# Two unused row gathers by GpSimd, placed late in a top-k search

## The chip, the cores and the metric

The kernel runs on one core of one Trainium2 chip. The metric is the device time of one execution in microseconds (us); lower is better. The core has five engines that run their own instruction streams and meet only at semaphores: TensorE (PE, with its weight loads PEld), VectorE (DVE), ScalarE (ACT), GpSimd (POOL) and SyncE (SP).

## The reference, cut to what matters

B=4 sequences of T=1024 tokens with C=256 channels go through a cross attention over 64 context tokens, and then through a layer of 8 experts in which each expert picks its own 256 tokens in each sequence:

```python
x = x + xattn(_layernorm(x), ctx, Wq, bq, Wk, bk, Wv, bv)
x = x + ffn(_layernorm(x), gate_w, w1, w2)

def ffn(x, gate_w, w1, w2):
    cap = int(2.0 * T / E)                      # 256
    probs = softmax(einsum('BTC,CE->BTE', x, gate_w))
    top_p, top_idx = lax.top_k(transpose(probs, (0, 2, 1)), cap)
    xin = take_along_axis(x[:, None], top_idx[..., None], axis=2)
    h = gelu(einsum('BElC,ECH->BElH', xin, w1), approximate=False)
    y = einsum('BElH,EHC->BElC', h, w2) * top_p[..., None]
    return zeros((B, T, C)).at[b_idx, top_idx].add(y)
```

## The kernel before, in words

The program has three stages.

**Attention (0 to about 52 us).** Eight groups of 512 tokens (`NG`) pass through scores, softmax and weighted values. The sum x + attention stays in the SBUF tile `x_all` and is stored to the output.

**Search and listing (about 58 to 86 us).** For each of 4 x 8 sequence-expert pairs the kernel finds the 256th largest probability by a search in 10 rounds of 3 bits each (`ROUNDS` is 5, run over the upper and then the lower bits), in two halves `h` of two sequences. A round goes back and forth between two engines: DVE compares all keys with 7 candidates (`compare`, line 1190, writes `over`), PE counts (line 872), DVE thresholds the count (`keep_reached`, line 1196), PE adds the new floor (line 880), DVE makes the next candidates (`candidates`, line 1201, writes `cand` and raises the semaphore `cand_ready[h]`). `candidates(0, ...)` is called four times in each block of five rounds, eight times in all. In the same stretch ACT normalises the rows, SP stores them to the DRAM scratch `xn_rows` (line 447, four DMAs, semaphore `xn_stored`), and ACT and DVE prepare the weights of expert 0 (`w1hi`, `w1lo`, `w2both`). Then DVE turns the thresholds into a list of row numbers `gidx` for expert 0 (lines 1294 to 1350).

**Experts (about 87 to 477 us).** Each expert works on 8 tiles of 128 rows, in two groups `g` of NL=4 tiles. GpSimd gathers the rows of a group by indirect DMA from `xn_rows` into `xg[g]` (line 525), PE turns them (line 750) into a PSUM bank, ACT and DVE split them into a high and a low part (`xhi`, `xlo`), PE multiplies with `w1` (lines 932 and 994) and `w2` (lines 944 to 953), and GpSimd adds the results to the output by indirect DMA (line 533). For the very first group the work starts on two of the four tiles: PE waits for `first_gathered` (2 tiles), later for the other two.

Every engine's order is the order in which the code issues; there is no scheduler. On GpSimd an instruction that waits holds up all that stands behind it on that engine. Between the setting of its last small tile (`own_base`, line 541) and its first gather GpSimd has two waits, for `xn_stored` and for `gidx_ready`, and nothing to do:

```python
pool.wait_ge(xn_stored, 16 * B)
pool.wait_ge(gidx_ready, 1)
for g in range(NU):
    gather(g, FIRST if g == 0 else 0)
```

On PE `keep_warm` issues transposes whose result nobody reads: 20 after the first list, 8 after the second ranking, 6 after the first turned rows.

Of the kernel before, what the change touches and what calls it, by code (L numbers as in the profile page):

```python
# [28 lines left out]
I32 = mybir.dt.int32  # L29
# [5 lines left out]
P = 128  # L35
# [10 lines left out]
def build(nc, x, xT, ctxT_in, Wq, WkT, Wv, WvT, bv, small, w1, w2, out):  # L46
    B, T, C = x.shape
    S = ctxT_in.shape[1] // B
    E, _, H = w1.shape
    CAP = 2 * T // E  # L50
    TC = T // P
# [19 lines left out]
    ROUNDS = BITS // RB  # L71
# [14 lines left out]
    out_v = out.rearrange("b (p c) d -> p b c d", c=TC)  # L86
    xn_v = xn_dram.rearrange("(b p c) d -> p b c d", b=B, c=TC)
    out_rows = out.rearrange("b t d -> (b t) d")

    with ExitStack() as stack:  # L90
        def sb(name, shape, dt):
            return stack.enter_context(nc.sbuf_tensor(name, shape, dt))

        def sem(name):
            return stack.enter_context(nc.semaphore(name))
# [81 lines left out]
        tok_val = sb("tok_val", [P, B, NB, TC], F16)  # L177
        onehot = sb("onehot", [P, B, SL, TC], F16)
        gidx = sb("gidx", [P, NB], I32)
        own = sb("own", [P, B, NB], F32)  # L180
        own_base = sb("own_base", [P, 1], F32)
        own_tok = sb("own_tok", [P, NB, B], F32)
# [6 lines left out]
        xg = [sb(f"xg{g}", [P, NL, CX], F32) for g in range(NU)]  # L189
# [46 lines left out]
        rows_stored = sem("rows_stored")  # L236
        rows_added = sem("rows_added")
        settled = sem("settled")
        xn_stored = sem("xn_stored")
        soft = sem("soft")  # L240
        normed = sem("normed")
# [9 lines left out]
        cand_ready = [sem(f"cand_ready{h}") for h in range(2)]  # L251
# [44 lines left out]
        pool_passed = sem("pool_passed")  # L296

        def keep_wait(eng, passed):

            eng.sem_inc(passed, 1)  # L300
# [162 lines left out]
        def _(pool):  # L463
# [23 lines left out]
            for r in range(ROUNDS):  # L487
# [3 lines left out]
                      channel_multiplier=0).then_inc(steps_set, 1)  # L491
# [36 lines left out]
            def scatter(g, e):  # L528
                for i in range(NL):
# [3 lines left out]
                    pool.indirect_dma_start(out=out_rows, out_offset=at, in_=ysb[g][:, i, :], in_offset=None,  # L533
                                            compute_op=ALU.add).then_inc(rows_added, 16)

            pool.memset(own[:], 0.0).then_inc(own_set, 1)
            pool.wait_ge(own_set, 1)
            for b in range(B):
                at = slice(b * SL, (b + 1) * SL)
                pool.memset(own[at, b], 1.0).then_inc(own_set, 1)  # L540
                pool.memset(own_base[at, :], float(b * T)).then_inc(own_set, 1)

            pool.wait_ge(xn_stored, 16 * B)
            pool.wait_ge(gidx_ready, 1)
            for g in range(NU):
# [959 lines left out]
```

## Time and profile before

| | us |
|---|---|
| median of 3 runs | 482.37 |
| lowest and highest of these | 482.18 and 506.92 |
| the profiled execution, its whole time | 479.12 |
| its span, from the first to the last instruction | 477.4 |

In the profiled execution 1.7 us lie around the span. Times of instructions below are from the start of the span. An indirect DMA of GpSimd shows in the engine's row only as long as GpSimd writes its descriptors; the time from issue to landing is another row. Matmuls are pipelined, so neighbouring PE rows overlap a little.

### The profile page before, as it was taken

Reading aid. Unit: us, or ns where it says so; the run is one execution under the profiler, and the core shown is the slowest. Engines: PE = TensorE matmul, PEld = TensorE weight load, DVE = VectorE, ACT = ScalarE, POOL = GpSimd, SP = SyncE. Lnnn points to the kernel's source line nnn. Section 1 sums busy time; section 2 is a strip of 40 time slices with the busy share of each in tenths; the row PEclk is TensorE's granted clock in tenths of the full one; section 3 lists DMA queues with packets and bytes.
Section 4 is the critical chain, followed back from the end, with each engine's and each line's share of the span. In section 5 each row is a group of like instructions: output and inputs, shape, how many; then the busy total and the mean of one; then the engine's idle time right before and its main releaser. Section 6 shows DMA issues by size and latency. Waiting matters only on the chain.

```text
span 477.4 us, 8390 instructions
## 1 busy us (share of the span) xinstructions
PE 443.9 (93%) x2600; PEld 376.3 (79%) x2600; DVE 317.9 (67%) x813; ACT 212.6 (45%) x523; POOL 198.4 (42%) x222
## 2 busy tenths in 40 slices
PE   8999344799999999999999999999999999999993
PEld 7887233788888888888888888888888888888993
DVE  3888798784677467746774677467656765674551
ACT  2478698042554255424532453345234524442331
POOL 4544400510835182518252815281538153814242
PEclk9999755799999999999999999999999999999998
DMA  8984844241425351625161517150715081504142
GB/s 275 362 279 154 287 185 183 57 157 55 80 56 152 72 80 50 178 53 78 45 194 42 84 34 212 30 84 28 219 34 78 23 220 38 85 12 45 13 49 29
DMA packets 35667, 52.46 MB, mean 110 GB/s; under 512 B 3009, under 2 KB 28994, under 8 KB 35138
## 3 DMA queue, kind: packets, MB, share of 16 engines
q1 hardware_dynamic: 22946, 34.89, 21.9%
q0 software_dynamic: 12288, 17.08, 21.1%
q10 hardware_dynamic: 416, 0.27, 0.2%
q8 instruction: 9, 0.15, 0.1%
q14 instruction: 8, 0.07, 0.0%
HBM read 35.17 MB, written 16.92 MB: 109 GB/s over the span
## 4 chain that ended last, share of the span: by engine, by line
PE 88%; DVE 8%; POOL 1%; ACT 1%; issue 1%; POOLq 0%; DVEq 0%
PE bank L932 37%; PE wide L949 23%; PE wide L953 12%; PE bank L750 4%; PE bank L811 3%; DVE over L1190 3%; PE wide L836 3%; PE wide L944 2%; PE bank L907 1%; DVE cand L1201 1%; DVE x_all L1106 1%; PE bank L755 1%; PE bank L994 1%; DVE w1lo L1370 1%; POOL rs L511 1%
## 5 line engine op out<-in xcount | busy, mean ns | idle before, releaser
L949 PE MATMUL wide<-w2both,hhi 128*128 128x512 f32 x480 | 176.1, 400 | 0.0
L533 POOL DMA_INDIRECT out_dram<-ysb,sidx x64 | 104.4, 1631 | 115.4 <-DVE ysb L1381 90.6
L689 ACT ACTIVATE hraw<-bank 128x512 f32<-128x512 f32 (+1 forms) x136 | 77.7, 571 | 132.6 <-PE bank L932 128.2
L953 PE MATMUL wide<-w2both,hlo 128*128 128x256 f32 x480 | 134.3, 280 | 0.0
L525 POOL DMA_INDIRECT xg<-xn_rows,gidx x64 | 65.5, 1023 | 132.3 <-issue 81.2
L1362 DVE CAST hhi<-hraw 128x512 fp32r<-128x512 f32 (+1 forms) x136 | 57.9, 425 | 79.4 <-ACT hraw L689 77.6
L949 PEld LDWEIGHTS wide<-w2both,hhi 128*128 128x128 f32 x480 | 90.5, 188 | 19.3
L1364 DVE TENSOR_TENSOR hlo<-hraw,hhi 128x512 fp32r<-128x512 f32 (+1 forms) x136 | 90.3, 664 | 4.7
L953 PEld LDWEIGHTS wide<-w2both,hlo 128*128 128x128 f32 x480 | 90.3, 188 | 3.5
L932 PE MATMUL bank<-xlo,w1hi 128*128 128x512 f32 (+1 forms) x268 | 80.5, 381 | 0.0
L932 PE MATMUL bank<-xhi,w1lo 128*128 128x512 f32 (+1 forms) x268 | 80.2, 380 | 0.0
L932 PE MATMUL bank<-xhi,w1hi 128*128 128x512 f32 (+1 forms) x268 | 79.9, 379 | 0.0
L932 PEld LDWEIGHTS bank<-xlo,w1hi 128*128 128x128 f32 x268 | 49.3, 188 | 10.3
L932 PEld LDWEIGHTS bank<-xhi,w1lo 128*128 128x128 f32 x268 | 49.3, 188 | 9.9
L932 PEld LDWEIGHTS bank<-xhi,w1hi 128*128 128x128 f32 x268 | 42.1, 188 | 5.6 <-ACT hraw L689 0.2
L682 ACT ACTIVATE xhi<-bank 128x512 fp32r<-128x512 f32 x30 | 18.0, 600 | 62.1 <-PE bank L750 62.1
L1354 DVE TENSOR_TENSOR xlo<-bank,xhi 128x512 fp32r<-128x512 f32 x30 | 20.8, 692 | 33.1 <-ACT xhi L682 31.7
L672 ACT ACTIVATE w2both<-raw 128x256 fp32r<-128x256 f32 x64 | 26.1, 417 | 23.3 <-PE wide L953 23.3
L1375 DVE TENSOR_TENSOR w2both<-raw,w2both 128x256 fp32r<-128x256 f32 x64 | 26.5, 420 | 4.8 <-ACT w2both L672 4.4
L1370 DVE TENSOR_TENSOR w1lo<-raw,w1hi 128x256 fp32r<-128x256 f32 x64 | 26.4, 422 | 0.0
L669 ACT ACTIVATE w1hi<-raw 128x256 fp32r<-128x256 f32 x64 | 25.8, 414 | 0.0
L1381 DVE SCALAR_TENSOR_TENSOR ysb<-wide,pcol,ysb 128x256 f32<-128x256 f32 x60 | 24.8, 477 | 0.0
(178 smaller groups left out, 435.3 us busy)
## 6 DMA issues: line engine op xcount, KB each, us to landing
raw<-in_w_dram SPq DMA_DIRECT2D x16, 1024.0 KB
xn_rows<-x_all SPq DMA_DIRECT2D x4, 1060.0 KB, 3.9
x_all<-in_x_dram SPq DMA_DIRECT2D x8, 512.0 KB, 9.6
raw<-in_x_turned_dram SPq DMA_DIRECT2D x8, 512.0 KB, 9.3
out_dram<-x_all SPq DMA_DIRECT2D x8, 512.0 KB, 4.9
xg<-xn_rows,gidx POOLq DMA_INDIRECT x64, 3.2
out_dram<-ysb,sidx POOLq DMA_INDIRECT x64
ctxT<-in_ctx_turned_dram ACTq DMA_DIRECT2D x1, 256.0 KB, 3.6
```

Of the source, the lines that this page charges most:

```text
L525: pool.indirect_dma_start(out=xg[g][:, i, :], out_offset=None, in_=xn_dram, in_offset=at).then_inc(first_gathered if i < first else gather ...
L533: pool.indirect_dma_start(out=out_rows, out_offset=at, in_=ysb[g][:, i, :], in_offset=None, compute_op=ALU.add).then_inc(rows_added, 16)
L669: act.activation(w1hi[:, j], w1raw[:, :, bass.ts(j, P)], ACT.Copy).then_inc(w1_hi, 1)
L672: act.activation(w2hi[:, j], w2raw[:, j], ACT.Copy).then_inc(w2_hi, 1)
L689: act.activation(hraw[s % 2][:, 0:width], bank[s % 2][:, 0:width], ACT.Gelu).then_inc(gelu_done, 1)
L932: t = pe.matmul(bank[s % 2][:, 0:width], w[:, j, k, :], xx[g][:, k, cols], start=(m == 0), stop=(m == 5))
L949: return pe.matmul(y[:, 0:2 * C], hhi[s % 4][:, at], w2both[:, j].rearrange("p a d -> p (a d)"), start=(j == 0), stop=(j == HC - 1), skip_ ...
L953: return pe.matmul(y[:, 0:C], hlo[s % 4][:, at], w2hi[:, j, :], start=False, stop=False, skip_group_check=True)
L1362: dve.tensor_copy(hhi[s % 4][:, 0:width], hraw[s % 2][:, 0:width]).then_inc(h_hi, 1)
L1364: dve.tensor_tensor(hlo[s % 4][:, 0:width], hraw[s % 2][:, 0:width], hhi[s % 4][:, 0:width].bitcast(F32), ALU.subtract).then_inc(h_split, 1)
L1370: dve.tensor_tensor(w1lo[:, j], w1raw[:, :, bass.ts(j, P)], w1hi[:, j].bitcast(F32), ALU.subtract).then_inc(w1_split, 1)
L1375: dve.tensor_tensor(w2lo[:, j], w2raw[:, j], w2hi[:, j].bitcast(F32), ALU.subtract).then_inc(w2_split, 1)
```

## The change

GpSimd sets a new tile `row_no` of 128 row numbers (0 to 127). After the small tiles it waits until that is set and until `cand_ready[0]` has reached 2 * (ROUNDS - 1) - 1 = 7, that is, until the seventh of the eight calls of `candidates(0, ...)` is done. Then it issues two indirect DMAs. Each gathers the rows 0 to 127 of the input x (1 KB each, 128 KB a DMA) into the first 256 columns of a slot of `xg[1]`, the buffer that the real gathers of the second group fill later. Nobody reads what the two have fetched. GpSimd then waits for both to land (`tried_out`), and only then stands before the two waits that it had already.

```diff
+    x_rows = x.rearrange("b t d -> (b t) d")
...
+        row_no = sb("row_no", [P, 1], I32)
...
+        row_set = sem("row_set")
+        tried_out = sem("tried_out")
...
+            pool.iota(row_no[:], [[0, 1]], base=0, channel_multiplier=1).then_inc(row_set, 1)
             pool.memset(own[:], 0.0).then_inc(own_set, 1)
             pool.wait_ge(own_set, 1)
             for b in range(B):
...
+            pool.wait_ge(row_set, 1)
+            pool.wait_ge(cand_ready[0], 2 * (ROUNDS - 1) - 1)
+            keep_wait(pool, pool_passed)
+            for i in range(2):
+                pool.indirect_dma_start(out=xg[1][:, i, 0:C], out_offset=None, in_=x_rows,
+                                        in_offset=bass.IndirectOffsetOnAxis(ap=row_no[:], axis=0)).then_inc(tried_out, 16)
+            pool.wait_ge(tried_out, 32)
             pool.wait_ge(xn_stored, 16 * B)
             pool.wait_ge(gidx_ready, 1)
             for g in range(NU):
```

GpSimd's instructions in the kernel before, from the last factor of the second normalisation to its first gathers; `[waits ...]` names the semaphores that hold a row up:

```order
L511 TENSOR_TENSOR rs<-ve,neghalf 128x2 [waits var2]
L536 MEMSET own 128x32
L540 MEMSET own 32x8 [waits own_set]
L541 MEMSET own_base 32x1
...
L525 DMA xg<-xn_rows,gidx 128x265 [waits xn_stored,gidx_ready]
L525 DMA xg<-xn_rows,gidx 128x265 x7
```

The same place on GpSimd in the changed kernel, whose lines are numbered up to 4 higher there:

```order
L515 TENSOR_TENSOR rs<-ve,neghalf 128x2 [waits var2]
L540 IOTA row_no 128x1
L541 MEMSET own 128x32
L545 MEMSET own 32x8 [waits own_set]
L546 MEMSET own_base 32x1
...
L552 DMA xg<-in_x_dram,row_no 128x256 [waits row_set,cand_ready0]
L552 DMA xg<-in_x_dram,row_no 128x256
L529 DMA xg<-xn_rows,gidx 128x265 [waits gidx_ready,tried_out,xn_stored]
L529 DMA xg<-xn_rows,gidx 128x265 x7
```

One IOTA and two DMAs are new, and the first real gather has one more semaphore to wait for. No row of PE, DVE, ACT or SP is added or moved.

## Rows read from the trace of the kernel before

**Rows 1.** The page: busy time of the engines, and the chain that ended last.

```profile
PE 443.9 (93%) x2600; PEld 376.3 (79%) x2600; DVE 317.9 (67%) x813; ACT 212.6 (45%) x523; POOL 198.4 (42%) x222
PE 88%; DVE 8%; POOL 1%; ACT 1%; issue 1%; POOLq 0%; DVEq 0%
```

**Rows 2.** All engines in order of time, 76 to 112 us: start, length, what.

```profile
76.21 0.28 DVE L1201 TENSOR_TENSOR cand<-bank,step_bits 128x112 int16<-128x112 f32 x1
...
85.61 0.27 DVE L1346 SCALAR_TENSOR_TENSOR own_tok<-bank,own_base,own 128x32 f32<-128x32 f32 x1 [0.62 <-PE bank L907]
85.92 0.19 DVE L1350 TENSOR_REDUCE gidx<-own_tok 128x8 int32<-128x32 f32 x1
...
87.07 1.49 POOL L525 DMA_INDIRECT xg<-xn_rows,gidx  x1 [30.74 <-DVE gidx L1350]
...
88.86 1.17 POOL L525 DMA_INDIRECT xg<-xn_rows,gidx  x1 [0.30 <-issue]
...
90.34 1.26 POOL L525 DMA_INDIRECT xg<-xn_rows,gidx  x1 [0.30 <-issue]
...
91.91 0.95 POOL L525 DMA_INDIRECT xg<-xn_rows,gidx  x1 [0.30 <-issue]
```

**Rows 3.** Line 525 (gathers), whole span: ns min/median/max; us from issue to landing.

```profile
L525 POOL DMA_INDIRECT xg<-xn_rows,gidx x64: 945/978/1493, 87.1 to 416.7; - x64
...
DMA to landing us min/median/max: 3.0/3.2/3.3
```

**Rows 4.** The last store of `xn_rows` (line 447), 75.0 to 75.4 us.

```profile
L447 SPq DMA_DIRECT2D xn_rows<-x_all x1: 319/319/319, 75.1 to 75.1; - x1
...
DMA to landing us min/median/max: 3.9/3.9/3.9
```

**Rows 5.** All engines in order of time, 117 to 119 us.

```profile
117.06 0.18 DVE L1350 TENSOR_REDUCE gidx<-own_tok 128x8 int32<-128x32 f32 x1
...
118.21 0.95 POOL L525 DMA_INDIRECT xg<-xn_rows,gidx  x1 [20.34 <-DVE gidx L1350]
```

**Rows 6.** The chain that ended last, 90 to 98.5 us: start, length, what.

```profile
92.97 0.22 DVE slot_of L1325
...
93.21 0.77 DVE xlo L1404 x2
```

**Rows 7.** Weight loads of PE in order of time, 90.5 to 96 us.

```profile
90.98 0.88 PEld L750 LDWEIGHTS wide<-identf 128*128 128x128 f32 x8
91.94 0.20 PEld L750 LDWEIGHTS bank<-identf,xg 128*128 128x128 f32 x2
...
94.97 0.24 PEld L750 LDWEIGHTS bank<-identf,xg 128*128 128x128 f32 x2
```

**Rows 8.** DVE's f16 comparison of line 1340, alike in form to the search's: ns min/median/max.

```profile
L1340 DVE TENSOR_TENSOR onehot<-slot_no,slot_of x9: 419/681/682, 84.0 to 385.7; 128x1024 f16<-128x1024 int16 x7, 128x512 f16<-128x512 int16 x2
```

**Rows 9.** All engines in order of time, 146 to 157 us.

```profile
146.71 1.62 POOL L533 DMA_INDIRECT out_dram<-ysb,sidx  x1 [10.15 <-DVE ysb L1381]
...
147.50 0.55 DVE L1362 CAST hhi<-hraw 128x512 fp32r<-128x512 f32 x1
...
150.53 1.55 POOL L533 DMA_INDIRECT out_dram<-ysb,sidx  x1 [0.31 <-issue]
...
150.97 0.68 DVE L1340 TENSOR_TENSOR onehot<-slot_no,slot_of 128x1024 f16<-128x1024 int16 x1
...
152.38 2.07 POOL L533 DMA_INDIRECT out_dram<-ysb,sidx  x1 [0.30 <-issue]
...
156.40 0.43 DVE L1362 CAST hhi<-hraw 128x512 fp32r<-128x512 f32 x1 [0.92 <-ACT hraw L689]
```

**Rows 10.** Stretches: length, busy of PE PEld DVE ACT POOL, PE clock, DMA share, GB/s.

```profile
78.00:79.00 1.00, 0.56 (x9) 0.40 (x9) 0.97 (x5) 1.00 (x5) 0.00 (x0) 0.50 0.51 195
...
88.00:89.00 1.00, 1.00 (x7) 1.00 (x6) 1.00 (x4) 0.00 (x0) 0.70 (x2) 0.54 0.00 0
89.00:90.00 1.00, 0.45 (x4) 0.22 (x2) 0.97 (x3) 0.00 (x0) 1.00 (x1) 1.00 0.50 136
```

**Rows 11.** GpSimd's small instructions, grouped by form: busy us, mean ns.

```profile
L490 POOL IOTA first_cand<- 128x112 int16 x1 | 0.2, 230 | 0.0
```

## The prediction

> **What bounds the kernel now.** I read the page first: PE is busy for 443.9 of 477.4 us and the chain that ended last is 88% PE and 8% DVE, with GpSimd at 1% [rows 1]. So a change on GpSimd costs or gives time only where DVE or PE waits for it. The reader should next look at the stretch that the change touches, in order of time [rows 2]. GpSimd sits idle for 30.74 us until DVE has the first list `gidx`, written at 85.92 + 0.19 = 86.11. The first real gather begins at 87.07. In the experts, from about 100 us on, PE is without a gap, and nothing that happens before 87 us reaches it but as a shift of that start. The question is therefore small and local: does the first expert start earlier or later?
>
> Two chains lead to that start. One is DVE's: after `gidx` it splits `w1`, then ranks the other seven experts, and only after `slot_of` at 92.97 does it reach the first `xlo`, at 93.21 [rows 6]. The other is the rows': the second gather is issued at 88.86 [rows 2]; gathers land 3.0 to 3.3 us after issue [rows 3], so at 91.9 or later, and PE's first weight load of gathered rows is at 91.94, straight behind eight warming transposes that began at 90.98 and filled 0.88 us, to 91.86 [rows 7]. So PE waited for rows for at most 0.08 us there, and what came next on the chain that ended last was DVE, not the rows [rows 6].
>
> **The change, part by part.**
>
> The IOTA. The nearest IOTA row has 0.23 us [rows 11]. It comes before `own` and ahead of a wait of 30.74 us [rows 2]. Cost on the path 0; without that idle time it would be the 0.23 us.
>
> The place of the two gathers. `cand_ready[0]` reaches 7 with the third candidate step of the second block, which ends at 76.21 + 0.28 = 76.49 [rows 2]. GpSimd takes time to wake: after `gidx` at 86.11 it starts at 87.07, 0.96 us later [rows 2]; one expert on, with the engine's gather code long in use, `gidx` ends at 117.06 + 0.18 = 117.24 and the gather starts at 118.21, 0.97 us later [rows 5]. So the delay is not a first-use cost and the change can't take it away; it also holds for the new wait. First new gather: 76.49 + 0.97 = 77.46.
>
> Their length. The shortest row of line 525 has 945 ns, the longest, the first, 1493 [rows 3]; the first three have 1.49, 1.17, 1.26, the fourth 0.95 [rows 2]. Taking 1.49 and 1.17 with 0.30 between: issue of the second at 77.46 + 1.49 + 0.30 = 79.25, written by 80.42, landed 79.25 + 3.3 = 82.55 by the longer landing. Bound from above by the longest indirect row that I show, a scatter of 2.07 [rows 9]: second issue 77.46 + 2.07 + 0.30 = 79.83, landing by 3.3 + (2.07 - 0.95) = 4.42, at 84.25. Both are before `gidx` at 86.11. So `tried_out` is no longer a wait when the list comes, by 1.9 to 3.6 us; cost 0. This cover is what the step lives on, and what it costs when it is gone is the second rival.
>
> Their data. They run beside the last store of `xn_rows`, issued at 75.1 and landed 3.9 us later, at 79.0 [rows 4]; in 78 to 79 us the DMA share is 0.51 [rows 10]. The two move 0.26 MB. Even if the store gave way to all of it at the 195 GB/s of that row, 1.3 us, it would land at 80.3, still 5.8 us ahead of the list. Cost 0.
>
> What their descriptor writing does to DVE, which is on the path in the search. Of two kinds of DVE work the trace has an example with GpSimd writing descriptors beside it. The f32 CAST took 0.55 us at 147.50, beside a scatter that began at 146.71 and took 1.62, and 0.43 us at 156.40 with none [rows 9]: 28% more. The f16 comparison of two SBUF tensors took 0.68 us at 150.97, inside the scatter of 150.53, and 0.681 or 0.682 in most of its uses (median and maximum), the one nearly alone included [rows 8, 9]: nothing more. The search's comparison has the second form (f16 from int16, TENSOR_TENSOR, both inputs in SBUF), and I take it: 0. The upper bound takes the CAST's 28% on all of the time of two writings, 1.49 + 1.17 = 2.66 us: +0.75 us.
>
> What the first real gathers gain. If being used before makes them short, 1.49 + 1.17 + 1.26 - 3 x 0.95 = 1.07 us go from the first three [rows 2], and the second is issued at 87.07 + 0.95 + 0.30 = 88.32, 0.54 us earlier. But at 91.94 - 0.54 = 91.40 PE is still in its eight transposes, and DVE is not ready for `xlo` before 93.21. The rows are not what is late; next in line is DVE's ranking, which nothing here shortens. The other two tiles: the fourth gather is issued 1.07 us earlier than at 91.91, but PE gets to them at 94.97 straight behind its multiplication of 94.72 [rows 2, 7]; from 91.91 + 3.0 = 94.91 to 94.97 no more than 0.06 us can have been waited. So the gain on the path is 0 to 0.1 us, 0.08 at the first place and 0.06 at the second at most; I take 0.
>
> What the descriptor writing suffers from DVE. The first three gathers are longer than the fourth, and DVE was at work beside all four; read so, 1.49 by 0.95 us, a factor of 1.6, is the worst that DVE did to a gather here [rows 2]. The times above hold it already. The Trainium skill ("SBUF — State Buffer", section "SBUF: two separate sides" and the one behind it) has a rule that speaks against the change: while DVE runs an operation that takes both ports, GpSimd is locked out and can't write descriptors, and a DMA of about 620 ns took about 3100 beside one. No row here shows a gather held up by a factor near that; what a hold of this kind would do is the second rival.
>
> **The sum.** IOTA 0, store 0, wait 0, search 0 (up to +0.75), first rows 0 (down to -0.1). So the profiled execution stays at 479.1 (span 477.4 and 1.7 around it), with -0.1 to +0.75. The median shown, 482.37, is 3.3 us above that execution, its lowest 482.18; I take the median as what the changed kernel is timed against: 482.4 + 0 = 482.4 us.
>
> **The rivals.**
>
> First rival, faster, the warmed gathers reach the path. All of the 1.07 us comes through, 481.3 us. It would need the rows to be what PE waits for at 91.94 and after; for it speaks that 91.9 and 91.94 are so close; against it that the chain that ended last has DVE's `slot_of` and `xlo` there, from 92.97 to 93.98, and not the rows [rows 6]. Were the -1.07 true it would show as an earlier `xlo`. Chance 0.08.
>
> Second rival, slower, the new wait takes the place of the old: the descriptors can't be written while DVE compares, the landing moves behind the list, and the real gathers, queued behind `tried_out` on GpSimd, move with it. The point from which it decides is 3.6 us of delay against my estimate of 82.55. DVE works without a pause in the search (0.97 of a us [rows 10]), and its longest pause ahead of the list is the 0.62 us before `own_tok`, from 85.61 - 0.62 = 84.99 [rows 2]. Were the writing held until then: first 84.99 + 1.49 = 86.48, second issued at 86.78, landed at 90.08, and with the wake-up of 0.97 the first real gather at 91.05 instead of 87.07: 4.0 us late. The rows come to PE at 95.9 instead of 91.94. `xlo` follows the turn by up to 93.21 - 91.94 = 1.27 us now, a part of which is DVE's ranking, so the start slips by 4.0 - 1.27 = 2.7 to 4.0 us. PE would have a pause, in which its clock can fall back from 2.4 to 1.2 GHz; it has come up from the lower level only in 88 to 89 us [rows 10]. If it spent 86.11 to 89.0, 2.9 us of work, once more at half speed, that costs 1.45. Together 482.4 + 2.7 to 482.4 + 5.5: 485.1 to 487.9. Against it: the real gathers beside a working DVE were never held that long [rows 2]. Chance 0.05. By the skill's figures alone, 3100 by 620, a writing of 0.95 us would be an estimated 4.75 us, and the rule would come out in the same region.
>
> Third rival, the descriptor writing slows the search by the CAST's share: 482.4 + 0.75 = 483.1 us. For it: the engines are known here to disturb each other in one form. Against: the form that matters was undisturbed. Chance 0.12.
>
> Fourth, the change doesn't do what it says: the semaphore passes at another step, or the gathers are as short as any other and warm nothing. Then the times are those of the forecast, and only the three rows of 1.49, 1.17, 1.26 would tell. It is part of the forecast.
>
> **How the numbers follow.** Forecast, no change that can be seen: 0.73. The first rival 0.08, the third 0.12, the second 0.05, and 0.02 for what I haven't thought of. A measurement of this kernel tells about 2%, 9.6 us, from no change; none of the cases reaches it: same 0.96; I leave 0.01 for faster and 0.03 for slower, where a lost clock level comes with the second rival. The range: the cases themselves span 481.3 to 483.1, but an execution of the same program can lie at 479.12, as the profiled one did, and the runs shown differ among themselves; so 479.5 at the low end, and at the high end 485.0, as the runs' other side and up to where the second rival begins.
>
> **What would show each step right or wrong.** In the changed kernel's trace: two rows of the new gather near 77.5 and 79.2 us, with the longer length at the first; DVE's comparisons at 380 to 390 ns around them as elsewhere; the first real gather 0.96 us after `gidx` as now, and then 0.95 us long if use warms, 1.49 if not; PE's first turn of rows still near 91.9 and `xlo` near 93.2. The prediction is wrong if the landing of the second new gather comes after the list, if the comparisons beside the new gathers grow, or if `xlo` moves with the rows.

## The result, and the profile after

The changed kernel took 483.97 us in the median of 22 runs (481.35 to 491.43), the kernel before 481.10 in the median of 22 runs beside them. The ratio is 1.005, 95% interval 1.0038 to 1.0062: about 2.4 us slower, far inside the 2% and yet not nothing. It leaves out four runs of the changed kernel and three of the kernel before, all at 489.9 us or above; the medians of all runs lie 2.9 us apart. The profiled execution took 482.82 us with a span of 481.1, 3.7 more than before's 477.4.

Of the page of the changed kernel, the two lines that answer to [rows 1]: busy time by engine, and the shares of the chain that ended last.

```profile
PE 444.0 (92%) x2600; PEld 376.5 (78%) x2600; DVE 317.9 (66%) x813; ACT 213.1 (44%) x523; POOL 199.9 (42%) x225
...
PE 86%; DVE 8%; ACT 1%; another core or an unknown queue 1%; POOL 1%; DMA 1%; issue 1%; POOLq 0%; SPq 0%; DVEq 0%
```

The two engines that lead the chain have no more work: PE is at 444.0 against 443.9 us and DVE at the same 317.9. GpSimd has 1.5 us more, the new gathers less what the real ones save, and it is at 1% of the chain. So 3.7 us of the span are pauses. One name in the chain is new, "another core or an unknown queue". There is only one core: it is a wait whose release the trace connects with no instruction.

The new gathers, by line, with their lengths (ns min/median/max) and landing times, and the search's comparisons beside them:

```profile
L552 POOL DMA_INDIRECT xg<-in_x_dram,row_no x2: 1195/1221/1247, 77.3 to 78.9; - x2
...
DMA to landing us min/median/max: 2.9/3.1/3.4
...
L1202 DVE TENSOR_TENSOR over<-key,cand x32: 380/388/394, 60.3 to 79.9; 128x448 f16<-128x448 int16 x32
```

They landed by 78.86 + 3.4 = 82.3, and the comparisons of DVE are as short beside them (380 to 394 ns) as elsewhere. Next, the changed kernel in order of time, 74 to 104 us (start, length, what, and in brackets the idle time before it and what ended it):

```profile
85.76 0.19 DVE L1362 TENSOR_REDUCE gidx<-own_tok 128x8 int32<-128x32 f32 x1
...
86.84 0.94 POOL L529 DMA_INDIRECT xg<-xn_rows,gidx  x1 [6.79 <-DVE gidx L1362]
...
88.09 1.03 POOL L529 DMA_INDIRECT xg<-xn_rows,gidx  x1 [0.30 <-issue]
...
89.43 0.95 POOL L529 DMA_INDIRECT xg<-xn_rows,gidx  x1 [0.31 <-issue]
...
90.68 0.95 POOL L529 DMA_INDIRECT xg<-xn_rows,gidx  x1 [0.30 <-issue]
...
92.50 0.39 ACT L720 ACTIVATE xhi<-bank 128x256 fp32r<-128x256 f32 x1 [11.53 <-PE wide L762]
...
93.20 0.42 DVE L1416 TENSOR_TENSOR xlo<-bank,xhi 128x256 fp32r<-128x256 f32 x1
...
93.94 0.39 ACT L720 ACTIVATE xhi<-wide 128x256 fp32r<-128x256 f32 x1 [1.06 <-remote]
...
95.88 0.95 POOL L529 DMA_INDIRECT xg<-xn_rows,gidx  x1 [0.31 <-issue]
95.90 0.38 PE L762 MATMUL bank<-identf,xg 128*128 128x128 f32 x2
...
98.34 0.39 ACT L723 ACTIVATE xhi<-bank 128x256 fp32r<-128x256 f32 x1 [4.01 <-remote]
...
100.11 0.60 ACT L701 ACTIVATE hraw<-bank 128x512 f32<-128x512 f32 x1 [1.11 <-PE bank L1006]
```

The same ACT rows in the kernel before, from its trace in order of time, 92 to 98 us:

```profile
92.42 0.39 ACT L708 ACTIVATE xhi<-bank 128x256 fp32r<-128x256 f32 x1 [11.19 <-PE bank L750]
92.70 0.38 ACT L708 ACTIVATE xhi<-wide 128x256 fp32r<-128x256 f32 x1
...
95.49 0.38 ACT L711 ACTIVATE xhi<-bank 128x256 fp32r<-128x256 f32 x1 [2.41 <-PE bank L750]
...
97.26 0.60 ACT L689 ACTIVATE hraw<-bank 128x512 f32<-128x512 f32 x1 [1.11 <-issue]
```

Read them in pairs. PE turns a 128-row tile of gathered rows by transposes, and ACT copies the turned tile out as `xhi`. The second copy began 0.28 us after the first in the kernel before, and 1.44 us after it now. The third began 95.49 - 95.07 = 0.42 us after PE's turn before, and 98.34 - 95.90 = 2.44 us after it now. Both late copies are marked "remote": ACT waited for PE's word, PE's transposes stand in the trace as done, and the word came late. The starts of PE's rows are recorded but their ends are modelled, so the rows do not tell a word that came late from a transposition that ended late. Counted from the start of the list `gidx`, the third copy is 9.57 us behind it before and 12.58 now, and the first GELU (`hraw`) 11.34 and 14.35: **3.01 us lost before the experts' stage is in its stride.**

A small second loss stands beside this one. The fifth gather now lies beside two operations of DVE that it did not touch before. First the kernel before, where the gather starts at 93.16, then the changed kernel:

```profile
92.83 0.22 DVE L1323 TENSOR_SCALAR block_of<-slot_any 128x224 int16<-128x224 int16 x1
92.97 0.21 DVE L1325 TENSOR_SCALAR slot_of<-slot_any 128x224 int16<-128x224 int16 x1
```

```profile
91.94 1.13 POOL L529 DMA_INDIRECT xg<-xn_rows,gidx  x1 [0.30 <-issue]
...
92.71 0.40 DVE L1335 TENSOR_SCALAR block_of<-slot_any 128x224 int16<-128x224 int16 x1
92.85 0.32 DVE L1337 TENSOR_SCALAR slot_of<-slot_any 128x224 int16<-128x224 int16 x1
```

Both sides are longer, DVE's 0.22 and 0.21 us become 0.40 and 0.32 and the gather takes 1.13 us instead of 0.94. So it is in all six traces in which the fifth gather starts 6.2 us behind the list (four runs of the changed kernel, two of the early one below); in the seven in which it starts 7.24 or 7.25 us behind it both operations take 0.22 and 0.21 us. The first `xlo`, next on DVE, comes 7.44 us behind the list instead of 7.29.

The other large piece is a fall of the clock. Stretches of the changed kernel (length, busy time of PE, PEld, DVE, ACT, POOL, the granted clock of PE as a share, DMA share, GB/s):

```profile
99.00:100.00 1.00, 0.95 (x7) 0.95 (x8) 1.00 (x4) 0.00 (x0) 0.00 (x0) 1.00 0.00 0
100.00:101.00 1.00, 1.00 (x8) 0.82 (x7) 0.78 (x3) 0.69 (x2) 0.00 (x0) 0.79 0.00 0
101.00:104.00 3.00, 3.00 (x8) 2.32 (x9) 2.93 (x8) 1.01 (x3) 0.00 (x0) 0.50 0.00 0
104.00:106.00 2.00, 2.00 (x12) 1.73 (x11) 1.86 (x5) 0.40 (x1) 0.00 (x0) 1.00 0.34 27
```

From about 100.6 to 104 us PE is fully busy at 0.50 of the clock, the lower of its two levels (1.2 of 2.4 GHz), behind its two pauses. In the kernel before the row of the same stretch is:

```profile
101.00:104.00 3.00, 3.00 (x18) 2.52 (x18) 2.56 (x7) 1.09 (x2) 0.00 (x0) 1.00 0.32 40
```

The fourth GELU starts 17.41 us behind the list before (103.33 less 85.92) and the same one 21.90 now (107.66 less 85.76): 4.49 later, of which 3.01 were lost already. The rest, **1.48 us**, I put down to the clock. It fits the stretch, since 3.4 us of work at half the clock would be 1.7 at the full one. From the list to the end of the span it is 391.48 us before and 395.34 now, 3.86 more; so **0.6 us came back** over the seven experts that follow. Where from, the tile experiment below shows.

### The profile page after: what moved, and what is told of

It is laid out like the page before. It is cut to its first block, busy times and chain, and to the rows that moved or that the text cites. A ratio compares the mean times of both kernels' runs of the same rounds, so it can differ in the third digit from the quotient of the medians.

```text
span 481.1 us, 8395 instructions
## 1 busy us (share of the span) xinstructions
PE 444.0 (92%) x2600; PEld 376.5 (78%) x2600; DVE 317.9 (66%) x813; ACT 213.1 (44%) x523; POOL 199.9 (42%) x225
## 4 chain that ended last, share of the span: by engine, by line
PE 86%; DVE 8%; ACT 1%; another core or an unknown queue 1%; POOL 1%; DMA 1%; issue 1%; POOLq 0%; SPq 0%; DVEq 0%
PE bank L944 37%; PE wide L961 23%; PE wide L965 12%; PE bank L762 3%; PE wide L848 2%; DVE over L1202 2%; PE wide L956 2%; PE bank L823 2%; DMA wq_sb<-in_Wq_dram 1%; PE bank L919 1%; DVE x_all L1118 1%; DVE cand L1213 1%; DVE w1lo L1382 1%; POOL rs L515 1%
```

## The experiments

The kernels ran in three sets: the first on one chip, which I call A, the second and third on another, B. So what differs between A and B can also be what differs between the sets. On which chip the result above was taken is not recorded. Each kernel is compared with the kernel before, run beside it.

**The changed kernel once more (chip A).** No edit.

> The changed kernel once more, for a second trace and a tight ratio. If the late release of ACT's xhi copies (1.4 us late at the second turn, 2.0 us late at the third and fourth in the first trace) belongs to the change, it is there again and the ratio is about 1.005. If it was a chance of that one execution, the copies follow the turns by 0.3 us and the loss must sit elsewhere.

It took 479.52 us against 480.13, ratio 0.9979 (0.9963 to 0.9995): here the change costs nothing and is a trifle faster (where the trifle comes from is told under the medians below). In order of time its trace has the same short gathers, with the copies on time:

```profile
88.32 0.94 POOL L529 DMA_INDIRECT xg<-xn_rows,gidx  x1 [6.78 <-DVE gidx L1362]
...
96.52 0.38 PE L762 MATMUL bank<-identf,xg 128*128 128x128 f32 x2
...
96.93 0.38 ACT L723 ACTIVATE xhi<-bank 128x256 fp32r<-128x256 f32 x1 [2.59 <-PE bank L762]
```

The third copy is 0.41 us behind its turn, the first GELU 11.47 us behind the list, and PE's clock does not fall there. So the instructions alone don't make the loss; it needs something that this set on chip A did not have. What is left there is 0.13 us at the first GELU (11.47 us behind the list against 11.34), the size of the longer `block_of` and `slot_of`. The next three kernels ran in the same set and could only show sizes, not the cause of the loss.

**The wait alone, without the gathers (chip A).** This kernel leaves out the two unused gathers, and with them the wait for their landing.

```diff
-            for i in range(2):
-                pool.indirect_dma_start(out=xg[1][:, i, 0:C], ...).then_inc(tried_out, 16)
-            pool.wait_ge(tried_out, 32)
```

> The changed kernel without its two gathers; the IOTA, the new tile and semaphores and the wait for the seventh candidate step stay. Theory A (the gathers warm GpSimd, the real ones come 0.5 to 1.1 us earlier and their landings fall on PE's turns): ratio 1.000, first real gather 1.49 us long. Theory B (the two extra DMAs leave something behind, whatever the timing): ratio 1.000 too. Theory C (the shift of code and semaphores): ratio stays at 1.005.

479.48 us, ratio 0.9986 (0.9972 to 1.0000). Its real gathers, in order of time:

```profile
86.72 1.52 POOL L529 DMA_INDIRECT xg<-xn_rows,gidx  x1 [30.58 <-DVE gidx L1358]
...
88.53 1.19 POOL L529 DMA_INDIRECT xg<-xn_rows,gidx  x1 [0.30 <-issue]
...
90.02 1.25 POOL L529 DMA_INDIRECT xg<-xn_rows,gidx  x1 [0.30 <-issue]
...
91.58 0.95 POOL L529 DMA_INDIRECT xg<-xn_rows,gidx  x1 [0.30 <-issue]
```

They are as long as before's 1.49, 1.17, 1.26 and 0.95 [rows 2], so it is the gathers of the change, not its wait, that make the first real one short. The first GELU came 11.37 us behind the list: the long gathers cost nothing, and the short ones of the run before gained nothing.

**The real gathers put back to their old time (chip A).** The new gathers stay; GpSimd does a small elementwise power (`pow` on 128x4 numbers, 1.06 us, its result unused) between the list and the first real gather.

```diff
             pool.wait_ge(gidx_ready, 1)
+            pool.tensor_tensor(spread[:], ve1[:, 0:GT], neghalf[:, 0:GT], ALU.pow)
             for g in range(NU):
```

> The changed kernel with one GpSimd operation of about 1.0 us between the arrival of the first list and the first real gather, so that the warmed gathers run about where the cold ones ran. Theory A: the late releases go away, ratio 1.000 to 1.002. Theory B and C: the delay changes nothing but the start of the rows, ratio 1.005 or up to 0.5 us more.

478.31 us, ratio 0.9975 (0.9963 to 0.9987), first GELU 11.34 us behind the list. In order of time:

```profile
86.11 1.06 POOL L557 TENSOR_TENSOR spread<-ve,neghalf 128x4 f32<-128x4 f32 x1 [6.07 <-DVE gidx L1363]
...
87.36 1.12 POOL L529 DMA_INDIRECT xg<-xn_rows,gidx  x1 [0.19 <-issue]
...
90.15 1.27 POOL L529 DMA_INDIRECT xg<-xn_rows,gidx  x1 [0.30 <-issue]
```

Two things show. The power started 0.18 us after the list (written at 85.93), where a gather that follows the same wait starts 0.9 us after it: the lag belongs to the gather, not to the semaphore. And the first three gathers take 1.12, 1.06 and 1.27 us. Whether the power undid some of the warming or the old places did it is not separated: the third gather takes 1.26 us unwarmed and 1.27 warmed when it starts 4.4 us behind the list, and 0.95 when it starts 3.7 us behind it. Only of the first, which starts within 0.1 us of its old place in the changed kernel (1.08 us behind the list against 1.15), is it shown that use makes it shorter.

**The new gathers 21 us earlier (chip A).** The wait for `cand_ready[0]` is left out, so they start 29.2 us ahead of the list instead of 8.5.

```diff
             pool.wait_ge(row_set, 1)
-            pool.wait_ge(cand_ready[0], 2 * (ROUNDS - 1) - 1)
             keep_wait(pool, pool_passed)
```

> The changed kernel without the wait for the seventh candidate step: the two gathers run at about 56 us, 30 us ahead of the real ones. Theory A if the warming lasts: as the changed kernel, 1.005, real gathers of 0.95 us; if the warming fades in 30 us, first real gathers of 1.2 to 1.5 us and ratio 1.000. Theory B: 1.005 whatever the length of the real gathers.

480.01 us, ratio 0.9990 (0.9977 to 1.0004). The real gathers were 0.94, 1.03, 0.95 and 0.95 us long, as in the changed kernel: what the use brings lasts through the 27.8 us in which GpSimd does nothing else. The first GELU came 11.48 us behind the list.

**The changed kernel a third time (chip B).** No edit.

> The changed kernel a third time. Its first run had a ratio of 1.005 and a trace in which PE's releases of ACT's xhi copies came 1.4 and 2.0 us late; its second had 0.998 and releases on time. If the late releases belong to some chips, they and a ratio above 1.003 come again on such a chip and not on others; if they are a matter of this change on every chip, 1.005; if they were chance, 0.998.

483.00 us against 479.14, ratio 1.0068 (1.0048 to 1.0089): the loss is back. So are the late copies; ACT in order of time, 97 to 100 us, where PE's turns began at 97.23 and 97.44:

```profile
99.58 0.38 ACT L723 ACTIVATE xhi<-bank 128x256 fp32r<-128x256 f32 x1 [3.93 <-remote]
99.86 0.38 ACT L723 ACTIVATE xhi<-wide 128x256 fp32r<-128x256 f32 x1
```

The first GELU is 14.47 us behind the list. From here on every kernel ran on chip B.

**The kernel before, in the changed kernel's place.** No edit: the noise between two sets of runs of one program.

> The kernel before, as a kernel of its own: ratio 1.000, and a trace of it from the same chip as the others of this call. From 16 GELUs to the next 16 (one expert) the first trace of before takes 46.93 us and all five traces with the new tile and semaphores take 46.84. If that is a matter of the chip, this run has what its neighbours have; if of the program, 46.93.

480.17 us, ratio 1.0007 (0.9992 to 1.0021), copies on time, first GELU 11.35 us behind the list. This execution of the kernel before on chip B has no late copy.

**The tile alone, and the semaphores alone.** Two edits of the kernel before, each once, with a profile.

```diff
         gidx = sb("gidx", [P, NB], I32)
+        row_no = sb("row_no", [P, 1], I32)
```

> The kernel before with the tile row_no alone (4 bytes a partition ahead of own, weights, rows and h), never written. If the shift of the later tiles makes the experts shorter by 0.09 us each, one expert takes 46.84 us here; if not, 46.93.

```diff
         settled = sem("settled")
+        row_set = sem("row_set")
+        tried_out = sem("tried_out")
         xn_stored = sem("xn_stored")
```

> The kernel before with the two semaphores row_set and tried_out alone, never used, which moves the numbers of those behind them by two. If these numbers make the experts shorter, one takes 46.84 us here; if not, 46.93.

478.13 and 480.33 us, both with copies on time (first GELU 11.35 and 11.34 us behind the list). So neither the 4 bytes nor the two semaphores brought the late copies, in one execution each. But the tile does something. The start of the third and of the eighth list in the kernel before:

```profile
163.92 0.19 DVE L1350 TENSOR_REDUCE gidx<-own_tok 128x8 int32<-128x32 f32 x1
...
398.66 0.19 DVE L1350 TENSOR_REDUCE gidx<-own_tok 128x8 int32<-128x32 f32 x1
```

the same two with the tile alone:

```profile
163.63 0.19 DVE L1351 TENSOR_REDUCE gidx<-own_tok 128x8 int32<-128x32 f32 x1
...
397.86 0.19 DVE L1351 TENSOR_REDUCE gidx<-own_tok 128x8 int32<-128x32 f32 x1
```

and with the semaphores alone:

```profile
165.21 0.19 DVE L1352 TENSOR_REDUCE gidx<-own_tok 128x8 int32<-128x32 f32 x1
...
399.98 0.19 DVE L1352 TENSOR_REDUCE gidx<-own_tok 128x8 int32<-128x32 f32 x1
```

Five experts take 234.74 us before (234.76 in the repeat), 234.77 with the semaphores, 234.23 with the tile, and 234.24 in the changed kernel (168.19 to 402.43). Declaring a tile of 4 bytes a partition ahead of the later ones is worth 0.1 us an expert. Over seven experts that accounts for the 0.6 us that came back. The likely reason is that every later tile moves by 4 bytes; the run shows the gain, not the reason.

**The decisive set, on chip B, which shows the loss.** A control first, the changed kernel a fourth time.

> The changed kernel as control on the chip of this call. So far: late releases and ratios 1.005 and 1.007 on two chips, none and 0.998 on a third. If this chip is of the first kind the releases of ACT's copies come 1.4 and 2.0 us late here again, and the three runs beside it can tell why; if not, 0.998 and nothing late in any of the four.

482.50 us against 479.99, ratio 1.0065 (1.0043 to 1.0088), all seven runs at 482.17 or more. This time the second copy was on time and the third was late all the same, PE's turns having begun at 94.90 and 95.11; ACT's row, and the stretch behind it:

```profile
98.03 0.38 ACT L723 ACTIVATE xhi<-bank 128x256 fp32r<-128x256 f32 x1 [5.31 <-remote]
```

```profile
100.00:103.00 3.00, 3.00 (x11) 2.52 (x10) 2.71 (x7) 1.30 (x3) 0.00 (x0) 0.50 0.00 0
```

Then the delayed kernel (the power between list and gathers, its edit shown above):

> The kernel with one GpSimd operation of 1.0 us ahead of the first real gather, which puts the warmed gathers where the cold ones ran. On a chip with late releases: theory A (the gathers' place against PE's turns decides) no late release and a ratio of 0.998 to 1.000; theory B (that the two gathers have run decides) releases late as in the control, ratio 1.005 to 1.007.

478.39 us, ratio 0.9972 (0.9954 to 0.9989). **The loss is gone from the median, with the new gathers still there.** In order of time:

```profile
87.28 1.13 POOL L529 DMA_INDIRECT xg<-xn_rows,gidx  x1 [0.19 <-issue]
...
92.91 0.95 POOL L529 DMA_INDIRECT xg<-xn_rows,gidx  x1 [0.30 <-issue]
...
95.24 0.38 ACT L724 ACTIVATE xhi<-bank 128x256 fp32r<-128x256 f32 x1 [2.48 <-PE bank L763]
```

Its fifth gather starts 7.25 us behind the start of the list; before it is 7.24 (93.16 less 85.92), in the changed kernel and its control 6.18 and 6.16. The third copy is on time, 0.41 us behind its turn at 94.83. In this one profiled execution (479.99 us, 1.6 above the median of the set) a smaller hold came further on: the first GELU is 13.07 us behind the list instead of 11.34. Eight of its twelve runs lie between 478.2 and 478.7, so this is not its usual time, and the clock stayed at 1.00 there.

Then the early kernel, whose real gathers are as short but whose new ones are long past:

> The kernel with the two new gathers at 57 us instead of 77 us, the real ones warmed all the same. On a chip with late releases: theory A late as in the control, ratio 1.005 to 1.007, since the real gathers stand at the same places; theory B in its form that the new gathers must be recent: none late, 0.998 to 1.000.

484.04 us, ratio 1.0083 (1.0052 to 1.0113), and the late copy again, PE's turns at 95.08 and 95.30:

```profile
86.87 0.94 POOL L529 DMA_INDIRECT xg<-xn_rows,gidx  x1 [27.83 <-DVE gidx L1361]
...
98.23 0.38 ACT L722 ACTIVATE xhi<-bank 128x256 fp32r<-128x256 f32 x1 [5.12 <-remote]
```

So how long ago the new gathers ran does not matter. What is left is where the real ones lie, or the power itself, which the delayed kernel has and this one has not. Last, the first four real gathers at their early times and the other four, which fetch the second group's rows, about 2 us later:

```diff
             for g in range(NU):
+                if g == 1:
+                    for idle in (spread, apart):
+                        pool.tensor_tensor(idle[:], ve1[:, 0:GT], neghalf[:, 0:GT], ALU.pow)
                 gather(g, FIRST if g == 0 else 0)
```

> The changed kernel with two GpSimd operations of 1.0 us each between the fourth and the fifth real gather, so that the second group's rows land some 2 us later. On a chip with late releases: if the landings of the second group's rows are what makes PE's releases of the third and fourth turn late, the delay of 2.0 us there goes away or moves while the 1.4 us at the second turn stays; if not, both stay. The second group's rows are then awaited at 102 us, for up to 1 us.

478.92 us, ratio 0.9980 (0.9964 to 0.9996), twelve of thirteen runs from 477.9 to 480.0. Its profiled execution took 488.04 us, 9 us more than the median of its set, so I compare no lengths of stages with it; the set of runs answers. In that trace the third copy starts 0.42 us behind its turn (105.04 against 104.62). With the first group's gathers warm and early the loss is absent, so it takes the second group's, gathers 5 to 8, in their early place, unless the powers themselves end it. I had expected a delay of 1.4 us at the second turn to stay; the runs leave no room for it, and the control and the early kernel lose their time without it.

The two kernels that end the loss on chip B both have powers of GpSimd that the other kernels lack. No run moves the gathers in another way, or adds a power and leaves them where they are, so place and power are not told apart.

**What a late copy waits for.** I put the late copies beside the DMA packets of the eighth gather. Stretches of the changed kernel, DMA share and GB/s last:

```profile
97.50:98.30 0.80, 0.00 (x0) 0.00 (x0) 0.00 (x0) 0.00 (x0) 0.00 (x0) 1.00 0.60 170
98.30:98.40 0.10, 0.00 (x0) 0.00 (x0) 0.00 (x0) 0.06 (x1) 0.00 (x0) 1.00 0.01 0
```

All engines stand still in the first, while the rows of the eighth gather come in at 170 GB/s; they end at 98.35 and ACT starts at 98.34. By the records of the packets the eighth gather's last data and the late copy stand at 99.70 and 99.58 in the third run of the changed kernel, 98.18 and 98.03 in the fourth, 98.32 and 98.23 in the early kernel on chip B. Four times within 0.15 us. The other holds do not end so. The second copy of the changed kernel starts at 93.94, in the midst of the fifth gather's rows (93.7 to 94.4), and the delayed kernel's first GELU at 98.73, in the midst of the eighth's (98.34 to 99.15). So this is a coincidence in time, not a mechanism: nothing in the program makes ACT's copy of the first group wait for the second group's rows, and in the kernel before the fifth to eighth gathers run over the same work with no such hold.

## Why the prediction held its range and missed the loss

**Point by point, what was right.** The new wait is none: the second new gather was issued at 78.86 (79.25 forecast) and landed by 82.3 (82.55), and GpSimd was free when the list came. The search is not slowed: 380 to 394 ns beside the writing, where the third rival asked for 28% more on some of them; 0 was right, 0.75 was not reached. The store ahead shows nowhere in the wait for the list. The first real gather began 86.84 - 85.95 = 0.89 us after the list was written (0.96 forecast). The first four real gathers are 0.94, 1.03, 0.95 and 0.95 us, 0.95 forecast for each; the fourth rival, that the new ones warm nothing, falls, though only for the first is it shown that warming and not its new place made it short. PE's first weight load of gathered rows is 5.95 us behind the list and was 6.02, so the rows gave the 0.07 us that the prediction allowed, but the first `xlo` is 7.44 behind it and was 7.29 [rows 6]. Nothing of the gathers' gain reached the path: the first rival falls too. Of the second rival, a longer landing behind DVE's work, nothing was seen: the new gathers took 1.25 and 1.20 us beside a DVE that never paused. The rule of the Trainium skill ("SBUF — State Buffer", section "SBUF: two separate sides") that stood beside that rival did not show with this form of DVE operation. The slowing of DVE that the third rival looked for in the search is there, but behind the list and in another form of operation: `block_of` and `slot_of` are why `xlo` moved by 0.15 us the wrong way.

**The step that failed** is "What the first real gathers gain": "So the gain on the path is 0 to 0.1 us". I gave the earlier gathers no effect but a gain. The other half, what goes wrong in the work that they now lie beside, had no term. Where the result was taken and on chip B it is a cost, by the copies that start late (3.01 us in the profiled execution after, 2.85 to 3.50 in the others that show it) and by the clock level lost behind PE's pauses (1.48 us). I had priced a lost clock level of 1.45 us, but under the second rival alone, which needed a late landing; here it came from early ones. The sum 0 was near the truth on chip A (0.9979) and wrong by 2.4 us where the result was taken.

**A second, smaller miss**: I took the experts as untouched, since no row of PE, DVE, ACT or SP moves in the order. But the tile `row_no` gave back 0.1 us an expert. That the forecast landed in its range was in part luck: the predicted 482.4 lies within 1.6 us of the median found, but the two misses have opposite signs, and the median I started from (482.37, of three runs) was itself 1.3 above the 481.10 of 22.

**What is shown and what is not.** Shown: the late copies are what the time went into, with the clock behind them; the loss goes when a power puts the real gathers back to their old places while the new gathers stay, and when two powers put the second group's alone later; it stays when the new gathers are moved 21 us away; the tile and the semaphores don't cause them. Not settled: what holds PE's word back; whether the later place of the gathers ends it or the powers that make the place; why the one set on chip A never showed it; and whether an execution that is not recorded would. All times here come from recorded executions, and a delay in a wait that ends with no known releaser could be one of the recording itself. No run could tell these apart.

**What the medians hide.** Leaving out the split kernel's, the first list starts at 85.6 to 85.9 us in eight profiled executions and at 87.1 to 87.4 in five, whichever the kernel. The times in the sets lie in two groups about 1.5 us apart as well. In the last set 12 of the 25 executions of the kernel before took 478.7 to 479.4 us and the other 13 took 479.99 or more, so its median of 479.99 lies at the edge between them, while eight of the delayed kernel's lie in the lower group. Matched by their times alone, lower with lower, the medians of the groups are 479.0 us before and 478.3 delayed on chip B, and 479.0 before, 478.4 changed and 478.2 delayed on chip A. That is 0.6 to 0.8 us where the tile gives 0.7 over seven experts, and next to nothing is left for the warmed gathers. So the ratios of 0.9972 and 0.9975 of the delayed kernel are no gain of the delay, and the loss on chip B is nearer to 3.5 us (482.5 against 479.0 in the fourth run of the changed kernel) than to the 3.1 of its ratio. None of this is a difference that a measurement of this kernel tells from no change at 2%.

## What to carry to other kernels

A cost of 0 for "the data only come earlier" covers the waits for the data, not the work that the transfers now run beside: give it a term on the slower side too. When a median moves but no engine's busy time does, list what the pauses end with, and repeat both kernels on a second chip before explaining; here chip A showed nothing. To test a suspected warming, keep the warming and put the warmed instructions back where they were, and run the delay once where it moves nothing, so that its own effect is known. Before taking a gain of a few tenths of a per cent from two medians, look whether the runs fall into groups.

## What the runs showed of the hardware that I had not expected

- GpSimd's first real indirect DMA here is long (1.49 to 1.52 us), and two unused ones ahead make it 0.94 at nearly the same place, even after 27.8 us of idle time between. With a small power just before it, and 0.5 us later, it is 1.12. The third stands with its place more than with use: 1.25 to 1.28 us when it starts 4.4 us behind the list, 0.95 at 3.7. The Trainium skill ("GPSIMD Engine Reference", section "2.1 Instruction dispatch") tells of about 6 us at the first call of a freshly loaded kernel; the first gather of this one is longer by 0.57 us at most, and whether its code was loaded then no run shows.
- After a semaphore of DVE a power starts on GpSimd within 0.18 us, an indirect DMA 0.89 to 0.97 us after it.
- A gather that lies beside DVE's int16 TENSOR_SCALAR operations lengthens them from 0.22 and 0.21 to 0.40 and 0.32 us and takes 1.12 or 1.13 us itself instead of 0.95, in six traces of six.
- A declared tile of 4 bytes a partition, never written, changes an expert by 0.1 us (234.74 against 234.23 us for five).
- A release of PE can reach ACT 2 to 3 us after its transposes stand as done, on chip B and where the result was taken; four of the longest of these ended within 0.15 us of the last packets of a gather that neither engine waits for.
- Kernels of every kind here, before and after, have executions whose first list is 1.5 us later (85.9 against 87.4 us in two profiles of the kernel before), with a granted clock of 0.62 instead of 1.00 in 16 to 20 us. Two profiled executions can thus differ by that much with no change at all; so I counted from the list.
